# Normalisation figures computed per expert slot and carried in the rows that are read back

## The chip, the cores and the metric

One core of a Trainium2 chip runs the whole kernel. The metric is device time in microseconds (us) of one execution; lower is better.

## The reference, cut to what matters

Two layers over x of shape (4, 1024, 128), 4096 tokens of width D = 128. The change is at the joint between the first layer's mixture of experts and the second layer's attention.

```python
x = x + attention0(layernorm(x))              # 16 heads, causal, ALiBi
n = layernorm(x)                              # router and experts, E = 8, capacity C = 512 per expert
gate, idx = max(softmax(n @ Wr + br))         # top 1; a token beyond C is dropped (its gate is 0)
x = x + gate * (relu(gate * n @ W1[idx] + b1[idx]) @ W2[idx] + b2[idx])
n = layernorm(x)                              # second layer's FIRST normalisation
x = x + softmax(tanh((n Wq)(n Wk)^T / sqrt(D))) n     # among the 4 tokens of one position t
n = layernorm(x)
x = x + n @ weight.T + pooled(n) @ disha
```

Here `layernorm(x) = (x - mean) / sqrt(var + eps)`, with no learned scale.

## The kernel before

Tokens lie in 32 tiles of 128 rows, in 8 chunks of `CH = 4` tiles. The kernel has four stages; the first (attention with its router preparation, up to about 500 us) is touched only in the width of rows.

**Routing (about 500 to 562 us).** `rows` holds for each token the gated, normalised input of its expert (XG), x after the first attention (X1) and its gate (GATE): 257 words. VectorE adds the attention's output chunk by chunk (`add`), takes mean and variance (`moments`), and after GpSimd's power (`power`, variance to the power -0.5) refines the root by one Newton step (`scales`). GpSimd sends each tile's rows to their slots in DRAM (`expert_rows`) by indirect DMA (`send_rows`, L1458). SyncE stores X1 as `x1_rows` once a chunk's `add` is done, waits for all of it (`x1_out`), and loads it back as `x2` (L1428), 32 DMAs, in an order in which the four tokens that attend to each other share a tile. Then it waits until all rows are scattered, and loads the 8 experts' slots (L1431) with `es_in`.

**Experts (562 to 590 us).** For each expert, 512 slots: TensorE transposes, multiplies by W1 and W2; VectorE adds the bias into `yb` (L1576) and makes `ye = yb * gate + x1` by four instructions (L1580), so `ye` is already x after the first layer. TensorE may run two experts ahead of VectorE (`yb_ready`). SyncE stores each expert's `ye` to `expert_out` (L1435).

**Last stage (590 to 676 us).** When all eight stores have landed (`y_out`), GpSimd gathers the rows of each chunk by four indirect DMAs (`fetch`, item "g", L1469) over `x2`; a dropped token's row is not fetched and keeps x1. The items of each chunk j, in order:

- m0 (VectorE): mean and variance of the four tiles (L1589, L1592, L1595), after `y_in[j]`
- p0 (GpSimd, L1477): power; n0 (VectorE, L1601 to L1605): Newton step, shift
- a0 (ScalarE, L1898): normalised rows into `xe`, up to XE = 4 chunks ahead of "mixed"
- t3, x3, u, ut, s (TensorE and ScalarE by turns): transposes and the products of the attention; te (ScalarE): tanh and exp; mask (VectorE, L1609)
- mixed (TensorE, L1814); mix (VectorE, L1616, L1621): weighted sum added to `x2`
- m1 (VectorE), p1 (GpSimd), n1 (VectorE): the second normalisation, the same lines as m0, p0, n0 but for the shift
- t4, x4, f: transposes and the last product (L1833); add (VectorE, L1631) into `res`, which SyncE stores (L1440). f(j) waits for add(j-1)

Each engine runs its items in one fixed order, `LAST_ORDER`. It is made before the program is built by `last_plan`: a list schedule over assumed durations (`STAGES`) with random trials. Assumed on TensorE are 6.85 us for a chunk's six items, on GpSimd 5.2 us for g and 1.05 us for each power. An item at the head of an engine's order blocks what stands behind it.

TensorE also runs products whose results nobody reads (`idle_work`, L1742): 6 before the experts, 18 after them, and 6 more after the first gathered chunk has landed. In each engine's program they stand ahead of what follows:

```python
        idle_work(psS, 18)
        pe.wait_ge(y_in[0], 16 * CH)
        idle_work(psS, 6)

        def t3(j):
            pe.wait_ge(xe_ready, j + 1)
```

## Time and profile before

| | |
|---|---|
| median of 3 runs | 681.1 us (679.51 to 681.44) |
| the profiled execution | 678.24 us, with a span of 676.0 us in the profile |
| TensorE busy, share of the span | 534.4 us, 79% |
| VectorE busy | 501.2 us, 74% |
| ScalarE busy | 418.7 us, 62% |
| GpSimd busy | 234.8 us, 35% |
| mean granted TensorE clock | 0.913 of 2.4 GHz |

The span runs from the first to the last instruction and DMA of the profiled execution; the execution's own time has 2.24 us more around it. Each row of a timeline groups instructions of one line that follow each other: start, duration, engine and line, operation, written tile <- read tiles, shape and count, and in brackets the idle time before and what ended it. "early" is the buffer that holds `x2` and the router's tiles, "issue" a wait that ends with nothing that the profile shows. A clock of 1.00 is 2.4 GHz, 0.50 is 1.2 GHz.

### The profile page before, as it was taken

To read this page: it belongs to the slowest core of one execution; us is meant where nothing else is said; L and a number is where in the kernel's file an instruction comes from. 1 tells how busy PE (TensorE), PEld (TensorE's weight loads), DVE (VectorE), ACT (ScalarE), POOL (GpSimd) and SP (SyncE) were. 2 spreads that over 40 slices of the span, in tenths; PEclk is the share of its full clock that TensorE was granted. 3 is DMA by queue.
4 is the path that set the end of the run, shared out by engine and by line. 5 is a ranking of instruction groups with operands and counts; after the bars stand their busy time and mean duration, and the time that the engine had idled before them with its cause. 6 is when DMAs were issued, how large, how long until landed. Compare 5 with 4: busy or idle time off the path is not lost. (4 is left out here: it accounts for less than half of the span.)

```text
span 676.0 us, 13740 instructions
## 1 busy us (share of the span) xinstructions
PE 534.4 (79%) x4905; PEld 251.8 (37%) x4905; DVE 501.2 (74%) x1035; ACT 418.7 (62%) x737; POOL 234.8 (35%) x333
## 2 busy tenths in 40 slices
PE   3774798899999899998898888988867617957774
PEld 1441233333233223333333233333127615835563
DVE  4999878889888888789895988889008732626796
ACT  1971278787887787787786767867861412316651
POOL 2563012212212215222323224621621671078821
PEclk9886599999999999999999999989998757976897
DMA  7379355466533353121340120401013247310122
GB/s 181 88 175 280 99 128 119 116 149 196 145 83 68 67 114 67 39 42 31 68 89 19 41 56 28 121 20 37 10 25 114 71 136 284 111 28 21 35 48 63
DMA packets 66891, 61.11 MB, mean 90 GB/s; under 512 B 12121, under 2 KB 56058, under 8 KB 66812
## 3 DMA queue, kind: packets, MB, share of 16 engines
q1 hardware_dynamic: 58100, 53.93, 31.6%
q0 software_dynamic: 2560, 3.38, 1.7%
q10 hardware_dynamic: 6164, 2.94, 1.6%
q8 instruction: 39, 0.64, 0.4%
q14 instruction: 28, 0.23, 0.1%
HBM read 33.03 MB, written 29.85 MB: 93 GB/s over the span
## 5 line engine op out<-in xcount | busy, mean ns | idle before, releaser
L933 DVE TENSOR_REDUCE neg_max<-bank 128x2 f32<-128x1024 f32 (+2 forms) x320 | 341.4, 1113 | 62.8 <-PE bank L829 60.0
L973 ACT ACTIVATE probs<-ring 128x512 f32<-128x512 f32 (+4 forms) x480 | 301.8, 682 | 73.6 <-PE ring L857 62.7
L857 PE MATMUL ring<-q_operand,k_operand 56*128 56x512 bf16 (+3 forms) x768 | 161.7, 331 | 18.7 <-ACT probs L973 13.9
L878 PE MATMUL sums<-probs,v_all 128*9 128x512 f32 (+3 forms) x1536 | 161.5, 493 | 6.6 <-POOL probs L1022 4.3
L1022 POOL TENSOR_SCALAR_AFFINE_SELECT probs<-probs 128x512 f32<-128x512 f32 x128 | 80.5, 634 | 210.8 <-ACT probs L973 210.4
L829 PE MATMUL bank<-k_operand,q_operand 54*128 54x512 bf16 (+3 forms) x768 | 141.4, 340 | 9.1 <-DVE v_all L613 5.3
L857 PEld LDWEIGHTS ring<-q_operand,k_operand 56*128 56x128 bf16 x768 | 49.4, 94 | 146.0 <-ACT probs L973 103.9
L823 PE MATMUL bank<-masks 64*128 64x128 bf16 (+2 forms) x768 | 70.9, 225 | 6.8 <-DVE neg_max L933 5.8
L829 PEld LDWEIGHTS bank<-k_operand,q_operand 54*128 54x128 bf16 x768 | 46.0, 97 | 26.7 <-DVE neg_max L933 15.1
L823 PEld LDWEIGHTS bank<-masks 64*128 64x128 bf16 x768 | 36.2, 96 | 40.9 <-DVE neg_max L933 27.2
L1469 POOL DMA_INDIRECT early<-expert_out,back x32 | 32.7, 1022 | 38.3 <-issue 38.3
L878 PEld LDWEIGHTS sums<-probs,v_all 128*9 128x9 f32 x1536 | 23.5, 88 | 55.5 <-issue 42.8
L1514 DVE TENSOR_TENSOR rows<-rows,bank 128x512 f32<-128x512 f32 x6 | 4.1, 684 | 36.2 <-PE bank L1674 33.6
L980 ACT COPY max_rows_sb<-ring 32x128 bf16<-32x128 bf16 x32 | 8.0, 251 | 35.3 <-PE ring L840 35.0
L1898 ACT ACTIVATE xe<-early,nt 128x128 f32<-128x128 f32 x32 | 13.2, 482 | 24.6 <-issue 18.8
L1458 POOL DMA_INDIRECT expert_rows<-rows,early x24 | 23.6, 982 | 8.4 <-issue 6.6
L1036 POOL CAST max_parts<-low_max 128x16 bf16<-128x16 f32 x16 | 3.1, 196 | 66.4 <-DVE low_max L938 66.4
L1477 POOL TENSOR_TENSOR rs<-ve,half_pow 128x4 f32<-128x4 f32 x16 | 17.3, 1082 | 20.9 <-DVE ve L1595 20.7
L1589 DVE BATCH_NORM_STATS2 stats<-early 128x6 f32<-128x128 f32 x64 | 13.9, 279 | 14.0 <-DMA early<-expert_out,back 13.8
L986 ACT COPY osum<-sums 128x512 f32<-128x512 f32 x32 | 18.8, 588 | 7.7 <-PE sums L878 7.4
L840 PE MATMUL ring<-identb,max_parts 128*32 128x128 bf16 x32 | 7.1, 222 | 19.8 <-POOL max_parts L1039 19.1
L1856 ACT COPY early<-ring 128x512 f32<-128x512 f32 x6 | 3.5, 585 | 25.3 <-PE ring L1685 16.8
(208 smaller groups left out, 657.5 us busy)
## 6 DMA issues: line engine op xcount, KB each, us to landing
q_operand<-q_rows SPq DMA_DIRECT2D x64, 96.0 KB, 3.8
k_operand<-k_rows SPq DMA_DIRECT2D x32, 192.0 KB, 4.5
q_rows<-early SPq DMA_DIRECT2D x36, 128.0 KB, 2.4
k_rows<-early SPq DMA_DIRECT2D x36, 128.0 KB, 2.4
expert_rows<-fill SPq DMA_DIRECT2D x16, 257.0 KB, 4.2
rows<-expert_rows SPq DMA_DIRECT2D x8, 514.0 KB, 6.6
weighted_sums<-osum SPq DMA_DIRECT2D x126, 18.0 KB
sums_in<-in_L_attn_x SPq DMA_DIRECT2D x4, 512.0 KB, 7.3
```

The source lines that it names most:

```text
L823: nc.tensor.matmul(ends, masks[rows, 0, a, :], masks[rows, 1, a:a + 1, 64 * a:P].to_broadcast([64, len(pairs), P - 64 * a]), start=a == 0, ...
L829: last = nc.tensor.matmul(ps[:, h, w * j:w * j + w], q_op[rows, buf, t // CH, p, P * (t % CH):P * (t % CH) + P], k_op[rows, buf, p, CW * k ...
L857: last = nc.tensor.matmul(psS[:, bank, w * j:w * j + w], k_op[rows, buf, p, P * kb:P * kb + P], q_op[rows, buf, c, p, q0:q0 + w], start=Tr ...
L878: last = nc.tensor.matmul(psO[32 * i:32 * i + HD + 1, q0:q0 + w], v_all[:, n, kb, i, :], probs[:, u % NPROBS, i // 2, i % 2, 0:w], start=u ...
L933: nc.vector.tensor_reduce(neg_max[:, n % 2, slot, kc, :, pairs[0]:pairs[-1] + 1, t % CH], src, AX.X, ALU.max, negate=True).then_inc(a_read, 1)
L973: nc.scalar.activation(dst, src, ACT.Exp).then_inc(ring_read, 1)
L986: nc.scalar.copy(osum[:, slot, :], psO).then_inc(o_ready, 1)
L1022: nc.gpsimd.affine_select(out=tri, in_=tri, compare_op=ALU.is_ge, fill=0.0, base=0, pattern=[[0, GH], [1, P]], channel_multiplier=-1).then ...
L1458: nc.gpsimd.indirect_dma_start(out=slots_dram, out_offset=bass.IndirectOffsetOnAxis(ap=slot[:, u:u + 1], axis=0), in_=rows[:, u, :], in_of ...
L1469: nc.gpsimd.indirect_dma_start(out=x2[:, u, :], out_offset=None, in_=y_dram, in_offset=bass.IndirectOffsetOnAxis(ap=back[:, u:u + 1], axis=0),
L1477: nc.gpsimd.tensor_tensor(rs[:, z, c], ve[:, z, c], half_pow[:, 0:CH], ALU.pow).then_inc(root_ready[z], 1)
L1589: last = nc.vector.bn_stats(stats[:, z, u, :], x2[:, u, :])
```

## The change

Mean and deviation of the second layer's first normalisation are no longer taken from the gathered rows in the last stage. For a token that an expert serves, VectorE computes them in the experts' stage from `ye`, per slot, in five groups of experts (`NORMS`), with a power per group on GpSimd (`root_of_slots`); scale and shift become two more words of each `ye` row, so the stored and gathered rows are D + 2 = 130 words. For a dropped token x is unchanged by the experts, and the router's own scale and shift serve (the two norms are of the same x1): they are written into `rows` as RS and MRS, and go out and back with X1. ScalarE's a0 reads both from `x2` and waits for the gather itself. m0, p0 and n0 leave the last stage, and `last_plan` makes a new order without them. The store of X1 waits for the chunk's `scales` in place of its `add`; the load of `x2` is 4 DMAs in place of 32; a group's stores wait for the group's scales. Smaller edits that follow (`x2` by its first D columns in `mix`, `add_out`, `t4`; the logits' scale read from `rows`) are left out below.

```diff
@@ -36,7 +36,7 @@
-XG, X1, GATE, ROW = 0, D, 2 * D, 2 * D + 1
+XG, X1, RS, MRS, GATE, ROW = 0, D, 2 * D, 2 * D + 1, 2 * D + 2, 2 * D + 3
@@ -312,8 +312,8 @@
-        x1_dram = nc.dram_tensor("x1_rows", (B * S, D), F32).ap()
-        y_dram = nc.dram_tensor("expert_out", (E * CAP, D), F32).ap()
+        x1_dram = nc.dram_tensor("x1_rows", (B * S, D + 2), F32).ap()
+        y_dram = nc.dram_tensor("expert_out", (E * CAP, D + 2), F32).ap()
@@ -341,8 +341,8 @@
-            xn2=part([TILES, D]), xt2=part([2, CW]), st=part([2, CW]), rdb=part([S]),
+            x2=part([TILES, D + 2]), xt2=part([2, CW]), st=part([2, CW]), rdb=part([S]),
@@ -1074,9 +1074,9 @@
-                    e_link(nc.gpsimd.tensor_tensor(root, t, root, ALU.mult))
-                    e_link(nc.gpsimd.tensor_tensor(u, r["mv2"][:, c, 0], root, ALU.mult))
-                    nc.gpsimd.tensor_scalar(r["nt2"][:, 2, c], u, -1.0, None, ALU.mult).then_inc(scales_ready, 1)
+                    e_link(nc.gpsimd.tensor_tensor(rows[:, c, RS], t, root, ALU.mult))
+                    e_link(nc.gpsimd.tensor_tensor(u, r["mv2"][:, c, 0], rows[:, c, RS], ALU.mult))
+                    nc.gpsimd.tensor_scalar(rows[:, c, MRS], u, -1.0, None, ALU.mult).then_inc(scales_ready, 1)
@@ -1315,16 +1315,15 @@
-        nc.vector.tensor_tensor(r["nt2"][:, 0, c], r["rs2"][:, c], gate[:, c], ALU.mult)
-        nc.vector.tensor_tensor(r["nt2"][:, 1, c], r["nt2"][:, 2, c], gate[:, c], ALU.mult)
+        nc.vector.tensor_tensor(r["nt2"][:, 0, c], self.rows[:, c, RS], gate[:, c], ALU.mult)
+        nc.vector.tensor_tensor(r["nt2"][:, 1, c], self.rows[:, c, MRS], gate[:, c], ALU.mult)
...
-    STAGES = [("g", "pool", 5200, [], None), ("landed", "lag", 1500, ["g"], None), ("m0", "dve", 1450, ["landed"], None),
-              ("p0", "pool", 1050, ["m0"], None), ("n0", "dve", 700, ["p0"], None), ("a0", "act", 1650, ["n0"], ("mixed", XE)),
+    STAGES = [("g", "pool", 5200, [], None), ("landed", "lag", 1500, ["g"], None), ("a0", "act", 1650, ["landed"], ("mixed", XE)),
@@ -1358,19 +1357,19 @@
-    ye = sb("ye", [P, E, CH, D])
-    x2 = xn2
+    ye = sb("ye", [P, E, CH, D + 2])
...
-    ve, rs, nt = sb("ve1", [P, 2, TILES]), sb("rs1", [P, 2, TILES]), sb("nt1", [P, 2, 2, TILES])
+    ve, rs, nt = sb("ve1", [P, 2, TILES]), sb("rs1", [P, 2, TILES]), sb("nt1", [P, 2, TILES])
+    NORMS = [(0, 1), (2, 3), (4, 5), (6,), (7,)]
@@ -1418,20 +1417,18 @@
-            sp.wait_ge(x1_ready, k + 1)
+            sp.wait_ge(scales_ready, 1 + [k in g for g in GROUPS].index(True))
...
-                         rows[:, CH * k:CH * k + CH, X1:X1 + D]).then_inc(x1_out, 16)
+                         rows[:, CH * k:CH * k + CH, X1:X1 + D + 2]).then_inc(x1_out, 16)
         sp.wait_ge(x1_out, 16 * CHUNKS)
-        for j in range(CHUNKS):
-            for q in range(B):
-                src = x1_dram[S * q:S * q + S, :].rearrange("(u t) d -> t u d", t=32)
-                sp.dma_start(x2[32 * q:32 * q + 32, CH * j:CH * j + CH, :], src[:, CH * j:CH * j + CH, :]).then_inc(x2_in[j], 16)
+        for q in range(B):
+            sp.dma_start(x2[32 * q:32 * q + 32, :, :], x1_dram[S * q:S * q + S, :].rearrange("(u t) d -> t u d", t=32)).then_inc(x2_in, 16)
         sp.wait_ge(scattered, 16 * TILES)
...
-            sp.wait_ge(ye_ready, e + 1)
+            sp.wait_ge(ye_ready, 1 + [e in g for g in NORMS].index(True))
@@ -1464,30 +1461,35 @@
                 pool.wait_ge(y_out, 16 * E)
-            pool.wait_ge(x2_in[j], 16 * B)
+                pool.wait_ge(x2_in, 16 * B)
...
                 nc.gpsimd.indirect_dma_start(
...
-        def root(z, j):
-            pool.wait_ge(ve_ready[z], j + 1)
+        def root(j):
+            pool.wait_ge(ve_ready, j + 1)
...
-            nc.gpsimd.tensor_tensor(rs[:, z, c], ve[:, z, c], half_pow[:, 0:CH], ALU.pow).then_inc(root_ready[z], 1)
+            nc.gpsimd.tensor_tensor(rs[:, 1, c], ve[:, 1, c], half_pow[:, 0:CH], ALU.pow).then_inc(root_ready, 1)
+        def root_of_slots(g):
+            pool.wait_ge(slot_ve, g + 1)
+            c = slice(CH * NORMS[g][0], CH * NORMS[g][-1] + CH)
+            nc.gpsimd.tensor_tensor(rs[:, 0, c], ve[:, 0, c], half_pow[:, 0:CH * len(NORMS[g])], ALU.pow).then_inc(slot_roots, 1)
         for name, i in ROUTE_ORDER:
...
+        for g in range(len(NORMS)):
+            root_of_slots(g)
         for name, j in LAST_ORDER:
...
-            elif name == "p0":
-                root(0, j)
...
-                root(1, j)
+                root(j)
@@ -1518,8 +1520,8 @@
-            link(nc.vector.scalar_tensor_tensor(rs2[:, c], nt2[:, 1, c], 1.5, rs2[:, c], ALU.add, ALU.mult))
-            nc.vector.scalar_tensor_tensor(nt2[:, 2, c], mv2[:, c, 0], -1.0, rs2[:, c],
+            link(nc.vector.scalar_tensor_tensor(rows[:, c, RS], nt2[:, 1, c], 1.5, rs2[:, c], ALU.add, ALU.mult))
+            nc.vector.scalar_tensor_tensor(rows[:, c, MRS], mv2[:, c, 0], -1.0, rows[:, c, RS],
@@ -1571,38 +1573,70 @@
-        for e in range(E):
+        def expert_sum(e):
             dve.wait_ge(y_psum, e + 1)
...
                                     b2b[:, e:e + 1, :].to_broadcast([P, CH, D]), ALU.add).then_inc(yb_ready, 1)
             dve.wait_ge(yb_ready, e + 1)
...
-                last = nc.vector.scalar_tensor_tensor(ye[:, e, a, :], yb[:, e % 2, a, :], es[:, e, a, GATE:GATE + 1],
+                last = nc.vector.scalar_tensor_tensor(ye[:, e, a, 0:D], yb[:, e % 2, a, :], es[:, e, a, GATE:GATE + 1],
...
-            last.then_inc(ye_ready, 1)
-        def moments(z, j):
+            last.then_inc(ye_sum, 1)
+        def slot_moments(e):
+            dve.wait_ge(ye_sum, e + 1)
+            for a in range(CH):
+                last = nc.vector.bn_stats(stats[:, 0, CH * e + a, :], ye[:, e, a, 0:D])
+            link(last)
+            for a in range(CH):
+                last = nc.vector.bn_aggr(mv[:, 0, CH * e + a, :], stats[:, 0, CH * e + a, :])
+            link(last)
+        def slot_variances(g):
+            c = slice(CH * NORMS[g][0], CH * NORMS[g][-1] + CH)
+            nc.vector.tensor_scalar_add(ve[:, 0, c], mv[:, 0, c, 1], EPS).then_inc(slot_ve, 1)
+        def slot_scales(g):
+            dve.wait_ge(slot_roots, g + 1)
+            es_of = slice(NORMS[g][0], NORMS[g][-1] + 1)
+            c = slice(CH * NORMS[g][0], CH * NORMS[g][-1] + CH)
+            v, r, t = ve[:, 0, c], rs[:, 0, c], nt[:, 0, c]
+            by_slot = lambda x: x.rearrange("p (e a) -> p e a", a=CH)
+            scale, shift = ye[:, es_of, :, D], ye[:, es_of, :, D + 1]
+            link(nc.vector.scalar_tensor_tensor(t, v, -0.5, r, ALU.mult, ALU.mult))
+            link(nc.vector.tensor_tensor(t, t, r, ALU.mult))
+            link(nc.vector.scalar_tensor_tensor(scale, by_slot(t), 1.5, by_slot(r), ALU.add, ALU.mult))
+            nc.vector.scalar_tensor_tensor(shift, by_slot(mv[:, 0, c, 0]), -1.0, scale, ALU.mult, ALU.mult).then_inc(ye_ready, 1)
+        for g, group in enumerate(NORMS):
+            for e in group:
+                expert_sum(e)
+                slot_moments(e)
+                if e == group[0] and g > 0:
+                    slot_scales(g - 1)
+            slot_variances(g)
+        slot_scales(len(NORMS) - 1)
+        def moments(j):
...
-                last = nc.vector.bn_stats(stats[:, z, u, :], x2[:, u, :])
+                last = nc.vector.bn_stats(stats[:, 1, u, :], x2[:, u, 0:D])
...
-                last = nc.vector.bn_aggr(mv[:, z, u, :], stats[:, z, u, :])
+                last = nc.vector.bn_aggr(mv[:, 1, u, :], stats[:, 1, u, :])
...
-            nc.vector.tensor_scalar_add(ve[:, z, t], mv[:, z, t, 1], EPS).then_inc(ve_ready[z], 1)
-        def scales_of(z, j):
-            dve.wait_ge(root_ready[z], j + 1)
+            nc.vector.tensor_scalar_add(ve[:, 1, t], mv[:, 1, t, 1], EPS).then_inc(ve_ready, 1)
+        def scales_of(j):
+            dve.wait_ge(root_ready, j + 1)
...
-            v, r, t = ve[:, z, c], rs[:, z, c], nt[:, z, 0, c]
+            v, r, t = ve[:, 1, c], rs[:, 1, c], nt[:, 1, c]
...
-            if z == 0:
-                nc.vector.scalar_tensor_tensor(nt[:, z, 1, c], mv[:, z, c, 0], -1.0, t, ALU.mult, ALU.mult).then_inc(nt_ready, 1)
@@ -1890,13 +1919,13 @@
-            act.wait_ge(nt_ready, j + 1)
+            act.wait_ge(y_in[j], 16 * CH)
...
-                last = nc.scalar.activation(xe[:, j % XE, i, 0:D], x2[:, u, :], ACT.Identity, bias=nt[:, 0, 1, u:u + 1],
-                                            scale=nt[:, 0, 0, u:u + 1])
+                last = nc.scalar.activation(xe[:, j % XE, i, 0:D], x2[:, u, 0:D], ACT.Identity, bias=x2[:, u, D + 1:D + 2],
+                                            scale=x2[:, u, D:D + 1])
...

```

## Rows read from the trace of the kernel before

**Rows 1.** Windows by stage: width, busy us (instructions) of each engine, granted clock, DMA.

```profile
560.00:590.30 30.30, 27.93 (x151) 22.14 (x152) 14.70 (x42) 10.07 (x16) 0.92 (x1) 0.91 0.56 212
590.30:640.60 50.30, 34.34 (x157) 25.18 (x155) 25.89 (x145) 22.62 (x48) 41.27 (x41) 0.76 0.12 28
640.60:676.00 35.40, 21.39 (x138) 17.55 (x138) 28.66 (x144) 13.04 (x26) 8.69 (x8) 0.88 0.23 53
```

**Rows 2.** Timeline of VectorE (DVE), experts' stage: start, duration, line, instructions.

```profile
571.07 0.69 DVE L1576 TENSOR_TENSOR yb<-ring,b2b 128x512 f32<-128x512 f32 x1 [7.21 <-PE ring L1767]
...
573.25 0.69 DVE L1576 TENSOR_TENSOR yb<-ring,b2b 128x512 f32<-128x512 f32 x1 [0.32 <-PE ring L1767]
...
585.57 0.68 DVE L1576 TENSOR_TENSOR yb<-ring,b2b 128x512 f32<-128x512 f32 x1
586.29 1.14 DVE L1580 SCALAR_TENSOR_TENSOR ye<-yb,rows 128x128 f32<-128x128 f32 x4
```

**Rows 3.** Timeline of GpSimd (POOL), last stage: gathers (L1469) and powers (L1477).

```profile
590.32 1.05 POOL L1469 DMA_INDIRECT early<-expert_out,back  x1 [29.40 <-issue]
...
595.59 1.00 POOL L1469 DMA_INDIRECT early<-expert_out,back  x1 [0.30 <-issue]
...
638.22 1.00 POOL L1469 DMA_INDIRECT early<-expert_out,back  x1 [0.31 <-issue]
...
647.88 1.38 POOL L1477 TENSOR_TENSOR rs<-ve,half_pow 128x4 f32<-128x4 f32 x1 [4.07 <-DVE ve L1595]
```

**Rows 4.** Waits of VectorE from 590.3 to 640.6: total us, times, longest.

```profile
DVE stats L1589 <- DMA early<-expert_out,back: 13.8, 2, 9.3
DVE nt L1601 <- POOL rs L1477: 10.6, 6, 3.3
```

**Rows 5.** Timeline of VectorE, end of the last stage.

```profile
653.75 1.12 DVE L1631 SCALAR_TENSOR_TENSOR res<-ring,nt,early 128x128 f32<-128x128 f32 x4
654.80 0.68 DVE L1609 TENSOR_TENSOR ee<-ee,samet 128x512 f32<-128x512 f32 x1
...
658.22 0.15 DVE L1601 SCALAR_TENSOR_TENSOR nt<-ve,rs 128x4 f32<-128x4 f32 x1
...
658.84 1.13 DVE L1631 SCALAR_TENSOR_TENSOR res<-ring,nt,early 128x128 f32<-128x128 f32 x4
...
671.35 1.12 DVE L1631 SCALAR_TENSOR_TENSOR res<-ring,nt,early 128x128 f32<-128x128 f32 x4 [0.74 <-PE ring L1833]
```

**Rows 6.** Timeline of VectorE, first chunk of the last stage.

```profile
596.76 0.87 DVE L1589 BATCH_NORM_STATS2 stats<-early 128x6 f32<-128x128 f32 x4 [9.33 <-DMA early<-expert_out,back]
...
598.09 0.17 DVE L1595 TENSOR_SCALAR ve<-mv 128x4 f32<-128x4 f32 x1
601.58 0.16 DVE L1601 SCALAR_TENSOR_TENSOR nt<-ve,rs 128x4 f32<-128x4 f32 x1 [3.32 <-POOL rs L1477]
...
602.25 0.86 DVE L1589 BATCH_NORM_STATS2 stats<-early 128x6 f32<-128x128 f32 x4
```

**Rows 7.** Timeline of SyncE's DMA queue: issues with their span.

```profile
542.15 19.14 SPq L1428 DMA_DIRECT2D early<-x_rows  x32
562.12 4.13 SPq L1431 DMA_DIRECT2D rows<-expert_rows  x8
```

**Rows 8.** Timeline of ScalarE (ACT), first chunk of the last stage.

```profile
602.37 1.65 ACT L1898 ACTIVATE xe<-early,nt 128x128 f32<-128x128 f32 x4 [18.81 <-issue]
```

**Rows 9.** Timeline of TensorE (PE), last stage.

```profile
596.78 5.49 PE L1742 MATMUL bank<-sel,ident 128*128 128x256 f32 x12 [4.25 <-DMA early<-expert_out,back]
...
607.33 2.07 PE L1804 MATMUL bank<-ut,xt 128*128 128x128 f32 x8 [0.68 <-issue]
...
612.49 1.07 PE L1814 MATMUL ring<-xe,ee 128*128 128x129 f32 x4
...
624.16 1.13 PE L1804 MATMUL bank<-ut,xt 128*128 128x128 f32 x8 [0.30 <-ACT th L1919]
```

**Rows 10.** Window of TensorE in the last stage: width, busy, granted clock, DMA.

```profile
606.00:608.00 2.00, 1.32 (x5) 0.57 0.14 33
```

More of the change, by code:

```diff
@@ L1275, in scaled @@
         n = c.stop - c.start
-        self.link(dve, nc.vector.tensor_tensor(lg, z, r["rs2"][:, c].unsqueeze(2).to_broadcast([P, n, E]), ALU.mult))
+        self.link(dve, nc.vector.tensor_tensor(lg, z, self.rows[:, c, RS].unsqueeze(2).to_broadcast([P, n, E]), ALU.mult))
         self.link(dve, nc.vector.tensor_tensor(lg, lg, w["brb"][:, :].unsqueeze(1).to_broadcast([P, n, E]), ALU.add))
@@ L1360, in later_stages @@
     at = sb("at", [P, 2, CW])
-    xn2, xt2, mv2, ve2, rs2, nt2, lg, ex, gate, slot, pos = (
-        r[k] for k in ("xn2", "xt2", "mv2", "ve2", "rs2", "nt2", "lg", "ex", "gate", "slot", "pos"))
+    x2, xt2, mv2, ve2, rs2, nt2, lg, ex, gate, slot, pos = (
+        r[k] for k in ("x2", "xt2", "mv2", "ve2", "rs2", "nt2", "lg", "ex", "gate", "slot", "pos"))
     router, place_counts = shared["router"], shared["place_counts"]
@@ L1392, in later_stages @@
         sem(n) for n in ("g_psum", "xgt_ready", "z_psum", "hid_ready", "y_psum", "yb_ready", "ye_ready", "y_out"))
-    x2_in, y_in = ([sem(f"{n}{j}") for j in range(CHUNKS)] for n in ("x2_in", "y_in"))
+    x2_in, slot_roots = sem("x2_in"), sem("slot_roots")
+    y_in = [sem(f"y_in{j}") for j in range(CHUNKS)]
     back_psum, back_ready = sem("back_psum"), sem("back_ready")
     fold_psum, fold_ready = sem("fold_psum"), sem("fold_ready")
-    ve_ready, nt_ready = [sem(f"ve_ready{i}") for i in range(2)], sem("nt_ready")
-    root_ready = [sem(f"root_ready{i}") for i in range(2)]
+    ve_ready, root_ready, slot_ve, ye_sum = sem("ve_ready"), sem("root_ready"), sem("slot_ve"), sem("ye_sum")
     xe_ready, t3_psum, xt3_ready, u_psum, ut_ready = (sem(n) for n in ("xe_ready", "t3_psum", "xt3_ready", "u_psum", "ut_ready"))
@@ L1620, in mix @@
                 c0 = (i % 2) * (CW // 2)
-                last = nc.vector.scalar_tensor_tensor(x2[:, u, :], psMix[i // 2][:, c0:c0 + D], inv[:, u:u + 1],
-                                                      x2[:, u, :], ALU.mult, ALU.add)
+                last = nc.vector.scalar_tensor_tensor(x2[:, u, 0:D], psMix[i // 2][:, c0:c0 + D], inv[:, u:u + 1],
+                                                      x2[:, u, 0:D], ALU.mult, ALU.add)
             last.then_inc(x3_ready, 1)
@@ L1630, in add_out @@
                 u = CH * j + i
-                last = nc.vector.scalar_tensor_tensor(res[:, j % 2, i, :], psOut[:, P * i:P * i + P], nt[:, 1, 0, u:u + 1],
-                                                      x2[:, u, :], ALU.mult, ALU.add)
+                last = nc.vector.scalar_tensor_tensor(res[:, j % 2, i, :], psOut[:, P * i:P * i + P], nt[:, 1, u:u + 1],
+                                                      x2[:, u, 0:D], ALU.mult, ALU.add)
             last.then_inc(res_ready, 1)
         for name, j in LAST_ORDER:
-            if name == "m0":
-                dve.wait_ge(y_in[j], 16 * CH)
-                moments(0, j)
-            elif name == "n0":
-                scales_of(0, j)
-            elif name == "n1":
-                scales_of(1, j)
+            if name == "n1":
+                scales_of(j)
             elif name == "mask":
@@ L1648, in _ @@
                 dve.wait_ge(x3_ready, j + 1)
-                moments(1, j)
+                moments(j)
             elif name == "add":
@@ L1822, in t4 @@
             for i in range(CH):
-                last = nc.tensor.transpose(psT4[:, P * i:P * i + P], x2[:, CH * j + i, :], ident[:, :])
+                last = nc.tensor.transpose(psT4[:, P * i:P * i + P], x2[:, CH * j + i, 0:D], ident[:, :])
             last.then_inc(t4_psum, 1)
```

4 lines of the change are left out of this document (2 added, 2 removed).

## The prediction

> **What bounds the kernel now.** I read first the windows by stage [rows 1]. The change touches the last two of them most: the experts' stage (to 590.3) and the last stage, which falls into a part with the gathers (to 640.6) and one after them. In the experts' stage TensorE is busy 27.93 of 30.30 us. In the gathers' part GpSimd is the busiest, 41.27 of 50.30, and VectorE has 25.89. After them VectorE has 28.66 of 35.40.
>
> Then the timelines, to see who waits. In the experts' stage VectorE starts at 571.07 and is back every 2.18 us, of which 0.32 is a wait for TensorE's last product [rows 2]: TensorE sets the pace, VectorE has 0.3 us of room per expert. The last `ye` ends at 587.43, and GpSimd's first gather starts at 590.32, 2.89 later, which is the last store [rows 2, 3].
>
> In the gathers' part GpSimd goes on without a pause: four gathers take 5.27 us, 1.32 each, and the last of 32 starts at 638.22 [rows 3]. That is 47.9 after the first, of which 31 x 1.32 = 40.8 are gathers and 7.1 are the seven powers among them, 1.0 each. VectorE waits here: 13.8 us for gathered rows in m0, 10.6 us for powers in n0 and n1 [rows 4]. So it has a backlog when the last rows land. From there it goes almost without a pause: add 1.05, then mask, mix and m1 3.42, then n1 0.62, in sum 5.09 a chunk [rows 5]. The last add ends at 672.47, and the stores bring the end, at 676.0, 3.5 later. The end is thus set by: last store of the experts, 32 gathers, VectorE's backlog.
>
> **What the change does before the experts.** X1 is stored after `scales` in place of `add`; from the first chunk's rows the way from m0 to the end of n0 is 5.6 us, a good bound for that delay [rows 6]. The 4 DMAs then issue far faster than the 32, which took 19.14 us of SyncE's queue from 542.15 to 561.3 [rows 7]. Behind them on the queue are only the experts' loads, issued at 562.12 when the scatter is done. If the data of the 4 loads need half the old 19.1 us they end about 557, and cost nothing; if they need all of it and start 5.6 late, they end at 566.9 and the experts' first load comes up to 5 us late, part of which TensorE's padding products there cover. I take nothing, and keep +3 for a rival. The Trainium skill (DMA: Bandwidth & Descriptors, How a descriptor splits into AXI transactions) says that a run not starting at a 256 B boundary costs extra beats, and 520-byte rows mostly do not; from its beats I would estimate some 25% on these loads, which the cover holds, and no row of before shows rows of 520 bytes. The 128 columns of VectorE's and ScalarE's tiles are as before, and two words more in a row of 257 are under 1%: nothing.
>
> **What it adds to the experts' stage.** Per expert, VectorE now spends 0.72 on `yb`, 1.14 on the four `ye`, 0.03 on its own semaphore, and then the moments of four tiles, which m0 shows at 1.33 (596.76 to 598.09) [rows 2, 6]. That is 3.22 against TensorE's 2.18, so VectorE sets the pace from its start at 571.07, with TensorE two experts ahead. Eight experts: 25.8 us, to 596.9. Five variance additions (at most 0.17 each, mostly overlapped): 0.5. Four sets of scales inside the loop at 0.67 (601.58 to 602.25): 2.7; their powers are done during the expert between. That makes 600.1. Then the last group, exposed: a power of 1.2 with its hops (between 1.0 and the 1.38 of [rows 3]), to 601.3, and four scale instructions, 0.8, to 602.1. With the same 2.89 for the store the first gather starts at 605.0, against 590.32: **14.7 us later**. Bounds: 13.5 (no own-semaphore gaps, short power) to 16.
>
> **What it takes from the last stage.** I count from the first gather, F. Before, the end is F + 85.7. Eight times m0 and n0 are 8 x (1.33 + 0.67) = 16 us of VectorE, and eight powers 8 of GpSimd; the long waits of VectorE [rows 4] lie mostly on them. The last rows now land at F + 43.3 plus 1.0 for each p1 that stands among the gathers (32 x 1.32, less the last gap, plus the 1.4 that the first chunk took to land: 590.32 to 596.76 less 5.0). With one or two p1 that is 44.8.
>
> The first chunk gets a new wait. The six padding products after `y_in[0]` ran from 596.78 to 602.27, beside m0, p0, n0 and a0, which ended at 604.02: they cost nothing [rows 8, 9]. Now only a0 (1.65) covers them, and the first t3 starts at F + 12, 3.8 us after its data. At the full clock they would take half, and 1.1 us would stay; but TensorE was idle for 4.25 before them and ran them at the half clock, and now it is idle longer. In the queue behind them is all of TensorE's work; GpSimd is not, so the gathers run on, and only as much of it remains as VectorE cannot make up.
>
> A chunk takes from the start of a0 to the end of m1: before, 602.37 to 613.56 for the last product of mixed, and mix and m1 2.8 more: 14.0 at the half clock (1.2 GHz); 12 at the full one (2.4 GHz), as s falls from 2.07 to 1.13 and mixed by as much [rows 8, 9]. Chunk j starts at F + 6.4 + 5.27 j. When the last rows land at 44.8, chunks 0 to 4 have mask, mix and m1 behind them and chunk 5 has mask and mix: 5 x 3.42 + 2.0 = 19.1 us of VectorE's work, with one or two pairs of n1 and add 21.6. Of 8 x 5.09 = 40.7 there remain 19.1. I add 2.5 for waits in this part (before, 31.9 us passed for 28.66 of work, some of it in the gaps that 5.09 holds) and the 3.5 of the stores: F + 69.9, and I take **F + 70.2** for an order that doesn't quite fit. This is the widest term: the new order is unknown to me, and a p1 must pass GpSimd's blocks of 5.2 us.
>
> **The sum**: 605.0 + 70.2 = 675.2 against the span of 676.0, a gain of 0.8 us: the 14.7 us added ahead of the gathers eat the 15.5 saved behind them. The profiled execution took 678.24, 2.24 over its span, and the median of the runs is 681.1; I carry the difference over, **680.3**. A change of under 0.3%, 2.0 us, can't be told from none in this kernel.
>
> **The rivals.** *Faster*: the order puts three or four p1 among the gathers, and VectorE keeps up, since it needs 5.09 a chunk and the gathers come every 5.27 or slower. Then the last chunk alone sets the end: its a0 starts at F + 46.3, m1 ends 12 later, p1, n1 and add take 3.1, the stores 3.5: 64.9, and 1.5 for meeting other chunks: 66.4. End 671.4, 4.6 less: 676.5. For it speaks that VectorE's waits on m0 and n0 go; against it that the seven powers before were let in only when due, and that a schedule which thinks TensorE the bound has no reason to serve p1 early.
>
> *Slower, by TensorE's clock*: in the window from 606 to 608 TensorE was busy 1.32 of 2.00 us and fell to the half clock with one chunk in work [rows 10]. After the change it works a new chunk every 5.3 us, with waits between. At the half clock the four items of a chunk that lead to mix (t3, u, s, mixed) take by my estimate 3.5 times s, 7.2 against 3.9 (s is 2.07 or 1.13 [rows 9]), more than the 5.27 of the gathers: 1.9 late per chunk. It decides from the third such chunk on: 5.8 late, some 2 of it made up, so 679 or 680, 3.5 to 4 more than the forecast's end: 684. Against it: after 640.6 TensorE was busy 21.39 of 35.40 and had a mean clock of 0.88 [rows 1]. The Trainium skill (TensorE: Matmul & The Clock Gate, HAM oscillation) has a rule for this: products in short bursts between waits for DMA restart cold each time. By that rule alone the half clock would stay through the gathers and this rival would hold; the trace agrees with it only in part, as the clock did rise later in the gathers' part, whose mean is 0.76.
>
> *Slower, by the loads of* `x2`: they land late, +3: 683.3; only if the four loads move their rows no faster than the thirty-two did, and start late besides.
>
> **How the numbers follow.** Forecast 0.40, with its own range 678 to 682.5 (the bounds of the experts' term, and one or two chunks' n1 and add more or less done at the landing); faster rival 0.31; clock 0.21; loads 0.08. The range reaches from 674.5 to 685. Faster by over 0.3% (below 679.1): 0.31 and a quarter of the forecast's, less a little for half-hearted cases, 0.40; slower (above 683.1): 0.28; the rest, 0.32, is the same.
>
> **What would show it.** In the profile after: VectorE's period in the experts' stage 3.2 to 3.6 us with no wait for TensorE; the first gather at 604 to 606; 12 padding records that end after a0 of chunk 0, and t3 behind them; the last gather at F + 42 to 45; VectorE's work after it, 19 us with the waits small. It would be wrong if VectorE's added work overlapped in the experts' stage better than its durations add up, if the new order stalls VectorE or TensorE behind a gather, or if the clock differs from what is said. It is most exposed in the last: an error of one chunk's work is 5 us, more than the whole difference.

## The result and the profile after

The changed kernel takes **694.1 us** (median of 4 runs, 692.4 to 696.0); the kernel before took 681.3 on the same chip. The ratio is **1.0214** (95% interval 1.0186 to 1.0241): 2.1% slower, above the range of the prediction. The profiled execution has a span of 690.3 us.

The part that the change adds came as forecast. VectorE in the experts' stage after; compare [rows 2] and [rows 6]:

```profile
568.88 0.69 DVE L1578 TENSOR_TENSOR yb<-ring,b2b 128x512 f32<-128x512 f32 x1 [7.86 <-PE ring L1796]
569.61 1.14 DVE L1582 SCALAR_TENSOR_TENSOR ye<-yb,rows 128x128 f32<-128x128 f32 x4
570.78 0.87 DVE L1589 BATCH_NORM_STATS2 stats<-ye 128x6 f32<-128x128 f32 x4
...
572.11 0.69 DVE L1578 TENSOR_TENSOR yb<-ring,b2b 128x512 f32<-128x512 f32 x1
...
599.59 0.17 DVE L1610 SCALAR_TENSOR_TENSOR ye<-mv,ye 128x4 f32<-128x4 f32 x1
```

An expert takes 3.23 us, without a wait for TensorE. GpSimd's first gather starts at 602.68, 33.80 us after the first `yb`, against 19.25 before [rows 2, 3]: 14.55 later, where I had 14.7.

The part that the change should shorten got longer. Windows after, cut at the first gather and at the end of the last one, as [rows 1]:

```profile
602.70:649.30 46.60, 26.29 (x112) 19.80 (x112) 7.55 (x33) 16.33 (x35) 33.46 (x33) 0.69 0.12 24
649.30:690.30 41.00, 27.14 (x172) 21.78 (x172) 31.50 (x151) 18.43 (x37) 8.24 (x8) 0.87 0.23 53
```

VectorE is busy only 7.55 us while the gathers run (25.89 before) and has 31.50 left afterwards, where I had reckoned 19.1 and some gaps. From the first gather to the end it takes 87.6 us, against 85.7 before and a forecast of 70.2. Who let VectorE wait is in its waits after, from 602 to 690:

```profile
DVE ee L1643 <- ACT ee L1953: 22.1, 3, 20.7
DVE inv L1650 <- remote: 18.0, 2, 13.4
```

The 20.7 is the first chunk's way to mask, which must be. The 13.4 is new: VectorE waits for the first mixed product, and the trace names no instruction that let it go ("remote"). The timelines of VectorE, ScalarE and TensorE around it:

```profile
620.46 0.69 DVE L1643 TENSOR_TENSOR ee<-ee,samet 128x512 f32<-128x512 f32 x1 [20.70 <-ACT ee L1953]
634.58 0.17 DVE L1650 RECIPROCAL inv<-bank 128x2 f32<-128x2 f32 x1 [13.43 <-remote]
```

```profile
636.75 0.60 ACT L1948 ACTIVATE th<-bank 128x512 f32<-128x512 f32 x1 [9.96 <-remote]
```

```profile
625.20 1.07 PE L1843 MATMUL ring<-xe,ee 128*128 128x129 f32 x4
626.06 1.91 PE L1833 MATMUL bank<-ut,xt 128*128 128x128 f32 x8
627.77 0.95 PE L1819 MATMUL bank<-ident,xe 128*128 128x128 f32 x4
636.03 1.12 PE L1852 MATMUL ring<-ident,early 128*128 128x128 f32 x4 [7.32 <-DVE early L1655]
```

By the records mixed of chunk 0 (L1843) ended at 626.27 and s of chunk 1 (L1833) at 627.97. VectorE learned of the first at 634.58, 8.3 us late, ScalarE of the second at 636.75, 8.8 late. I call this a **held signal**: a consumer idle until "remote", though the product it waits for is recorded as ended.

"Remote" says more than that: the trace also has the time of each update of a semaphore, and the word stands where such an update ended the wait and no instruction that makes it had ended near it. The update for mixed of chunk 0 stands at 634.55, the one for s of chunk 1 at 636.73. So the consumers started at once, and the updates themselves were late. Only TensorE's are: from 500 us on, those of ScalarE, VectorE and GpSimd stand within 0.04 us of their instructions' ends in all the traces here, beside the same gathers. GpSimd meanwhile:

```profile
602.68 1.11 POOL L1466 DMA_INDIRECT early<-expert_out,back  x1 [3.72 <-issue]
...
632.78 1.00 POOL L1466 DMA_INDIRECT early<-expert_out,back  x1 [0.30 <-issue]
637.59 1.05 POOL L1474 TENSOR_TENSOR rs<-ve,half_pow 128x4 f32<-128x4 f32 x1 [3.81 <-DVE ve L1631]
```

From 602.68 to 633.78 it issued 24 gathers with 0.30 us between them. Before, a power p0 (L1477) stood behind every fourth or eighth [rows 3]. The change took p0 out, and the two signals came 0.8 and 3 us behind the end of that run.

### The profile page after: what moved, and what is told of

Same layout as the page of the kernel before. It is cut to its first block and busy times, and to the rows that moved or that the text cites. A ratio compares the mean times of both kernels' runs of the same rounds, so it can differ in the third digit from the quotient of the medians.

```text
span 690.3 us, 13701 instructions
## 1 busy us (share of the span) xinstructions
PE 533.3 (77%) x4905; PEld 250.7 (36%) x4905; DVE 499.4 (72%) x1020; ACT 417.9 (61%) x737; POOL 234.1 (34%) x330
## 5 line engine op out<-in xcount | busy, mean ns | idle before, releaser
L857 PE MATMUL ring<-q_operand,k_operand 56*128 56x512 bf16 (+3 forms) x768 | 161.0, 330 | 19.1 <-ACT probs L973 13.9
L1927 ACT ACTIVATE xe<-early 128x128 f32<-128x128 f32 x32 | 13.2, 486 | 26.4 <-DMA early<-expert_out,back 26.4
L1036 POOL CAST max_parts<-low_max 128x16 bf16<-128x16 f32 x16 | 3.2, 197 | 66.4 <-DVE low_max L938 66.4
L1771 PE MATMUL bank<-sel,ident 128*128 128x256 f32 x48 | 14.3, 469 | 11.4 <-DMA early<-expert_out,back 11.4
L840 PE MATMUL ring<-identb,max_parts 128*32 128x128 bf16 x32 | 7.1, 222 | 19.7 <-POOL max_parts L1039 19.1
L1643 DVE TENSOR_TENSOR ee<-ee,samet 128x512 f32<-128x512 f32 x8 | 5.5, 687 | 22.1 <-ACT ee L1953 22.1
L1474 POOL TENSOR_TENSOR rs<-ve,half_pow 128x4 f32<-128x4 f32 x8 | 9.3, 1157 | 29.6 <-DVE ve L1631 29.6
```

The lines of the kernel that those rows point to most:

```text
L857: last = nc.tensor.matmul(psS[:, bank, w * j:w * j + w], k_op[rows, buf, p, P * kb:P * kb + P], q_op[rows, buf, c, p, q0:q0 + w], start=Tr ...
L1771: nc.tensor.matmul(bank[:, CW // 2:], ident[:, :], sel[:, 0:2, :].rearrange("p c m -> p (c m)"), start=True, stop=True)
L1927: last = nc.scalar.activation(xe[:, j % XE, i, 0:D], x2[:, u, 0:D], ACT.Identity, bias=x2[:, u, D + 1:D + 2], scale=x2[:, u, D:D + 1])
```

## The experiments

**Theory S**: TensorE's signals are held while GpSimd issues indirect DMAs without a pause, and p0 had been the pause. **Rivals**: **O**, the newly planned order of the last stage; **C**, TensorE's half clock and the padding products behind `y_in[0]`. Ratios are to the kernel before. "Stage" is the time from the first gather to the end, "held" the sum of VectorE's and ScalarE's waits that end in "remote" in it (whole waits, so it can be more than the signals were late), "runs" the gathers between pauses of at least 0.9 us in their issue. Of 'after' they are 87.6, 32.8 and 24, 8; of the kernel before 85.7, 2.4 and 8, 8, 4, 4, 4, 4.

The experiments ran in five batches, each on a chip of its own with the kernel before beside it: e1 to e4 on chip 13, e5 to e8 on 10, e9 to e12 on 4, e13 to e16 on 9, e17 and e18 on 12. The chip matters, as will be seen.

**Pauses in the changed kernel, and the two rivals alone.**

```python
            if name == "g":
                fetch(j)
                nc.gpsimd.tensor_tensor(brk[...], brk[...], half_pow[:, 0:CH], ALU.pow)   # e1
...
-        pe.wait_ge(y_in[0], 16 * CH)      # e2
-        idle_work(psS, 6)
...
-LAST_ORDER = last_plan()                 # e3: before's order, less m0, p0, n0
```

> The changed kernel with one extra GpSimd power on 4 scratch columns behind each chunk's 4 gathers (8 in all, about 1.05 us each). Theory S (held signals): TensorE's finish signals reach VectorE and ScalarE late while GpSimd issues indirect DMAs without a break, and the change made one run of 24 gathers out of runs of at most 8 to 10. With runs of 4 the wait of 13.4 us before the first reciprocal of the mix (VectorE, L1650) falls to 3 to 7 us, that of te(1) on ScalarE goes, and the time falls from 694 to 684 to 689 us, though GpSimd has 8 us more to do. Theory O (the new order of the last stage) and theory C (TensorE at half clock, uncovered padding): the waits stay, the gathers end up to 8 us later, 694 to 699 us.

> The changed kernel without the wait of TensorE for the first rows and the six padding products behind it. Theory C: t3(0) comes 3 to 4 us earlier, and if the products' time is what the first chunk lacks, the time falls by 3 to 4 us to 690 to 691 us. Theory S: mixed(0) may end earlier, but its signal is still held to the end of the run of gathers at F+31, so the time stays within 1.5 us of 694.

> The changed kernel with the last stage's order of the kernel before (without its m0, p0 and n0) in place of the newly planned one. Theory O: the planned order costs most of the 17 us, so the time falls to 680 to 684 us. Theory S: the first run of gathers has 20 in place of 24 and ends 5 us earlier, so the held signal of mixed(0) comes about 5 us earlier; 689 to 692 us.

Measured: e1 **1.0146** (1.0103 to 1.0189), e2 **1.0280** (1.0229 to 1.0330), e3 **1.0346** (1.0306 to 1.0387). VectorE at the same two places in e1:

```profile
621.74 0.69 DVE L1648 TENSOR_TENSOR ee<-ee,samet 128x512 f32<-128x512 f32 x1 [20.56 <-issue]
624.29 0.17 DVE L1655 RECIPROCAL inv<-bank 128x2 f32<-128x2 f32 x1 [1.86 <-PE ring L1848]
```

The wait of 13.43 is 1.86, with no held signal in the stage (81.1 us), although GpSimd has 8.4 us more to do. Neither rival gains anything alone: e2's interval overlaps that of the change (1.0186 to 1.0241), e3 lies above it. In e3, where the first run has 20 gathers and the second 12, another signal is held:

```profile
650.59 1.13 DVE L1674 SCALAR_TENSOR_TENSOR res<-ring,nt,early 128x128 f32<-128x128 f32 x4 [17.75 <-remote]
```

The product of this wait is recorded as ended at 644.56 and its update stands at 650.48, 5.9 us later; the rest of the 17.75 is the work before it, which had been held too. I had expected e3 to gain some us by its shorter first run; it lost another 9.

**The reverse, on the kernel before.** Both kernels put 1.0 in place of the root of the first normalisation, which is what their output leaves out.

```python
             elif name == "p0":
-                root(0, j)                                                  # e4: nothing here
+                nc.gpsimd.tensor_tensor(brk[...], brk[...], half_pow[:, 0:CH], ALU.pow)   # e9
```

> The kernel before with the eight powers of the first normalisation left out on GpSimd (VectorE takes 1.0 in place of the root; the sum of products is then wrong by that part, nothing else is left out). This takes 8.4 us from GpSimd and a round trip from each chunk. Without theory S: 2 to 5 us faster than before (676 to 679 us). Theory S: the gathers now stand in one run of 20 or more as in the changed kernel, the waits for TensorE's signals grow to 8 us or more, and the time is 681 to 690 us, no faster or slower than before although work was taken away.

> The kernel before with the root of the first normalisation replaced by 1.0 as in the run without its powers (the product is wrong by that part), but with a power of the same size on scratch columns where each p0 stood, which waits for nothing. GpSimd has the work and the breaks of the kernel before, without the round trip. Theory S2: the gathers stand in runs of at most 12 between pauses of 1 us again, and the 1.3% that leaving the powers out had cost is gone: 674 to 680 us against 679.5 of the kernel before, its last stage (first gather to end) 80 to 86 us in place of 95.4. If it was the earlier gathers or the missing round trip that cost the time, and not the missing pause, it stays at 685 to 690 us.

Measured: e4 **1.0127** (1.0088 to 1.0165), e9 **1.0025** (0.9997 to 1.0053). Taking GpSimd's eight powers out, work and round trip both, makes the kernel before slower: stage 95.4, held 27.0. With a power on scratch, which nobody waits for, the time is that of the kernel before: 86.8, held 0.0. But e9 ran on chip 4, where, as shown below, no signal was held in any kernel; it can't show that its powers freed anything, and e4 has no control on its own chip but the kernel before. VectorE in e4:

```profile
621.18 0.17 DVE L1618 RECIPROCAL inv<-bank 128x2 f32<-128x2 f32 x1 [4.40 <-remote]
...
640.29 0.17 DVE L1618 RECIPROCAL inv<-bank 128x2 f32<-128x2 f32 x1 [6.26 <-remote]
```

**How long a pause, and how many.** In the changed kernel a memset of one column, and a power behind chunk 4 only:

```python
                fetch(j)
+                nc.gpsimd.memset(brk[:, 0, j:j + 1], 1.0)      # e5; e8: in fetch, behind every gather
...
+                if j == 4:                                     # e6
+                    nc.gpsimd.tensor_tensor(brk[...], brk[...], half_pow[:, 0:CH], ALU.pow)
```

> As the run with a power behind each chunk's gathers, but the break is a memset of one column (about 0.1 us) in place of a power of 1.05 us. If any other instruction of GpSimd lets the held signals through (S1), mix(0) starts within 3 us of mask(0)'s end, as with the powers, and since GpSimd has 7.5 us less to do the time falls to 683 to 688 us. If it is the pause of about 1 us in the issue of transfers that does it (S2), mix(0) waits 8 to 13 us as in the changed kernel, and the time is 692 to 696 us.

> A memset of one column behind every gather (32 in all), otherwise the changed kernel. S1 (any other GpSimd instruction lets the signals through): no wait for TensorE's signals is longer than 2.5 us, GpSimd gets 3 to 6 us longer, time 684 to 689 us. S2 (a pause of about 1 us is needed): waits of 8 us and more remain, 694 to 699 us.

> The changed kernel with a single power on scratch columns, behind the gathers of chunk 4 (runs of 20, 4 and 8 gathers). Theory S: the power stands at about F+26 to F+27 (F is the start of the first gather), so mix(0) starts at F+27 to F+28.5 in place of F+31.9, and the time falls by 3 to 5 us to 689 to 692 us. Theories without S: mix(0) does not move against mixed(0)'s end, time 694 to 696 us.

Measured: e5 **1.0226** (1.0196 to 1.0257), e8 **1.0249** (1.0230 to 1.0267), e6 **1.0226** (1.0204 to 1.0248). The memset of 0.11 us fits into the 0.30 us that lie between two gathers anyway, as GpSimd's timeline of e5 shows:

```profile
612.29 1.00 POOL L1467 DMA_INDIRECT early<-expert_out,back  x1 [0.30 <-issue]
613.29 0.11 POOL L1495 MEMSET brk<- 128x1 f32 x1
613.59 1.00 POOL L1467 DMA_INDIRECT early<-expert_out,back  x1 [0.19 <-issue]
```

e5 differs from e1 by that instruction alone (in place of a power of 1.05 us), and both chips hold signals. So another instruction is not enough; the issue must pause. In e6 the power stood at 631.00 to 632.05 and mix(0) started at 633.30, F + 28.2, as forecast, against F + 31.9 after the change; but nothing was gained. One pause doesn't free all that is held: s of chunk 1 and t3 of chunk 2 had ended at 627.98 and 628.42, before the power, and their updates stand at 638.96 and 641.79, behind the next one. VectorE's next mix waited 7.3 us more.

**The order, with pauses.** The last stage is planned anew with 6.25 us for a chunk's gathers instead of 5.2; e13 has this order and no pause.

```python
-    STAGES = [("g", "pool", 5200, [], None), ...      # e7, e10, e12, e13; e14 keeps 5200
+    STAGES = [("g", "pool", 6250, [], None), ...
...
                fetch(j)
+                nc.gpsimd.tensor_tensor(brk[...], ..., ALU.pow)     # e7; e12, also without the padding
+                nc.gpsimd.memset(brk[...], 1.0)                     # e10, e14: 256 columns, 0.33 us
```

> Powers as breaks behind each chunk's gathers, and the last stage's order planned anew with 6.25 us in place of 5.2 us for a chunk's gathers. The held signals gone, what is left is the order: VectorE waits 8.0 us for ee and 4.3 us for roots after 624 in the run with the breaks alone. If order O matters beside S, 683 to 686 us; if not, 688 to 689 us as with the breaks alone.

> The replanned kernel with its breaks, without the wait of TensorE for the first rows and the padding products behind it. With the signals no longer held, t3(0) comes 3 to 4 us after a0(0)'s rows instead of behind the products. Theory C: the first chunk gains 3 to 4 us and the time falls to 679 to 681 us. If the later chunks are bound by GpSimd's gathers (6.25 us each, to F+50) and VectorE, or the clock falls for want of the products, it stays at 682 to 685 us.

> The replanned kernel with the breaks shortened from 1.05 us to a memset of 256 columns, estimated at 0.55 us (512 columns took 1.005 us, one column 0.11 us). If half a microsecond of pause is enough, no wait for TensorE's signals over 3 us, GpSimd ends 4 us earlier, and 679 to 683 us against 683.2. If it needs about 1 us, the waits of 8 us and more are back and it takes 688 to 695 us.

> The replanned order of the last stage alone, with no break between the gathers: runs of 24, 4 and 4 gathers as in the changed kernel. If the pauses do it (S), the wait for mixed(0) or a later product of 8 us or more is back and the time is 688 to 697 us (ratio to the kernel before 1.012 to 1.025). If it is the order (O), no such wait, and the time is that of the run with the short breaks, 674 to 678 us (ratio 0.995 to 1.002).

> The changed kernel's own order with the short breaks (a memset of 256 columns, 0.33 us, which waits for the one before it). S: mix(0) waits under 3 us instead of 13.4, and since GpSimd has 5.8 us less in breaks than with the powers (ratio 1.0146), the ratio to the kernel before is 1.002 to 1.010. If the order was what the replanned runs gained by, the waits stay and the ratio is 1.018 to 1.025.

Measured: e7 **1.0067** (1.0035 to 1.0099), e12 **1.0106** (1.0057 to 1.0155), e10 **0.9972** (0.9945 to 1.0000), e13 **1.0233** (1.0183 to 1.0282), e14 **1.0233** (1.0181 to 1.0286).

With pauses the order is worth 5.8 us of the stage (81.1 in e1, 75.3 in e7); without them it is worth nothing (e13: 90.7, held 24.6). So O holds only behind S. Taking the padding products out gains nothing in either setting: C falls in that part. e10's stage is 69.3 us with no held signal, within 1 us of the 70.2 that I had forecast for the change, though with another order and on chip 4. Against e12 on the same chip (75.2, without the padding products) it is 5.9 less, and its eight pauses take 8 x (1.05 - 0.33) = 5.8 less of GpSimd: that gain is saved work, not freed signals. Its waits of VectorE, to be set against those of after:

```profile
DVE ee L1649 <- ACT ee L1959: 20.3, 1, 20.3
DVE inv L1656 <- PE ring L1849: 5.4, 3, 2.3
DVE nt L1643 <- POOL rs L1475: 1.3, 1, 1.3
```

e14 shows the late signals best, as they start there under the full clock. Its window, then ScalarE:

```profile
624.80:632.60 7.80, 4.05 (x26) 3.15 (x26) 3.61 (x16) 3.77 (x8) 6.37 (x7) 1.00 0.13 26
```

```profile
631.35 0.60 ACT L1954 ACTIVATE th<-bank 128x512 f32<-128x512 f32 x1 [2.78 <-remote]
...
634.23 0.59 ACT L1944 COPY xt<-bank 128x512 f32<-128x512 f32 x1 [1.63 <-remote]
...
637.08 0.59 ACT L1964 COPY xt<-ring 128x512 f32<-128x512 f32 x1 [2.26 <-remote]
```

The three products that these wait for are recorded at 627.13 to 629.71, one behind the other; their updates stand at 631.33, 634.21 and 637.06, 2.9 us apart, in order. At the next pause of GpSimd (its last gather of that run ended at 651.66) they come at once. TensorE, then the two that waited:

```profile
647.57 0.61 PE L1849 MATMUL ring<-xe,ee 128*128 128x129 f32 x4
648.02 1.05 PE L1839 MATMUL bank<-ut,xt 128*128 128x128 f32 x8
```

```profile
652.89 0.17 DVE L1656 RECIPROCAL inv<-bank 128x2 f32<-128x2 f32 x1 [6.59 <-remote]
```

```profile
652.98 0.60 ACT L1954 ACTIVATE th<-bank 128x512 f32<-128x512 f32 x1 [1.69 <-remote]
```

The second product alone is eight matmuls, 1.05 us; the two signals are 0.09 us apart. In the changed kernel four updates stand at 650.34, 650.43, 650.53 and 650.59, for products recorded as ended from 645.86 to 648.58. So the products were done and the news of them was late, not TensorE slow. The Trainium skill (Perfetto Trace Analysis, Tensor Engine Instruction) fits with it: TensorE's end in a trace is an estimate, and the update is pushed only when PSUM has acknowledged the writes, and then has to spread. It gives no delay of microseconds, and no tie to GpSimd; the runs show both.

**Fewer and shorter pauses, and the chip.** e15 is e10, and e16 the kernel before, with one memset among the routing's scatters. e11, e17 and e18 are e7 with fewer powers.

```python
             send_rows(u):
+                if u == KB + 3:                           # e15, e16
+                    nc.gpsimd.memset(rest[:, :], 1.0)
...
                fetch(j)
+                if j % 2 == 1:      # e11; e17: j in (1, 3); e18: j == 3
+                    nc.gpsimd.tensor_tensor(brk[...], ..., ALU.pow)
```

> The replanned kernel with short breaks, and one more memset of 256 columns behind the fourth of the eight scatters that GpSimd issues in a row in the routing part (525 to 536 us in the kernel before, where ScalarE waited 8.5 us at L1856 and VectorE 2.5 us at L1514 for signals of TensorE). S: those waits fall by 3 to 5 us, of which 0 to 3 us reach the end, since the second half of the routing is bound by GpSimd's 16 scatters: ratio 0.993 to 0.998.

> The kernel before with that one memset of 256 columns behind the fourth of the eight scatters, and nothing else changed. S: the waits of 8.5 us (ScalarE, L1856) and 2.5 us (VectorE, L1514) for signals of TensorE at 537 us fall by 3 to 5 us; ratio 0.995 to 1.000. Without S: the waits stay, and the scatters come 0.3 us later.

> The replanned kernel with powers only behind chunks 1, 3, 5 and 7: runs of 8 gathers, as the kernel before had at most, in place of 4. Theory S2: a signal can now be held up to 10 us; GpSimd has 4.2 us less. Where the signals of the first two chunks fall decides; 683 to 690 us, with one to three waits of 3 to 8 us for TensorE's signals.

> The replanned order with powers of 1.05 us as breaks behind chunks 1 and 3 alone: GpSimd's own powers p1 follow from chunk 5 on, so no run has more than 8 gathers. Theory S2 (what counts is that a pause of about 1.2 us comes at least every 8 to 12 gathers): no wait for held signals, and 2 us less of GpSimd than with breaks behind chunks 1, 3, 5 and 7 (ratio 1.0016): ratio 0.996 to 1.001. If every further pause was needed, a hold is back and the ratio is over 1.005.

> The same with one power, behind chunk 3: runs of 16, 8, 4 and 4 gathers. The first chunk's signals that were held in the runs of 20 and 24 fall at F+18 to F+25 (F is the start of the first gather), just about this break at F+21, so if pauses only free what is held, the holds are short: 0 to 4 us in sum, ratio 0.996 to 1.006. If a hold, once begun in a long run, goes on behind the pause, waits of 8 us or more are back and the ratio is 1.010 to 1.025.

Measured: e15 **1.0179** (1.0141 to 1.0218), e16 **1.0009** (0.9985 to 1.0033), e11 **1.0016** (0.9990 to 1.0042), e17 **1.0125** (1.0084 to 1.0166), e18 **1.0251** (1.0207 to 1.0295). The memset among the routing's scatters frees nothing (ScalarE's wait of 8.5 us is 8.5 in both). e15, which differs from e10 by that one instruction and its tile, has held signals again: ScalarE, 9.00 us to 633.84. It also ran on another chip, and the routing tells which of the two counts. There ScalarE waits beside eight scatters that the change and the experiments leave alone (but for two words more in a row, and e15's and e16's memset); the kernel before, then e10:

```profile
537.15 0.58 ACT L1856 COPY early<-ring 128x512 f32<-128x512 f32 x1 [8.49 <-remote]
```

```profile
532.09 0.59 ACT L1891 COPY early<-ring 128x512 f32<-128x512 f32 x1 [3.17 <-PE ring L1720]
```

In all sixteen traces of the other chips this wait is 8.3 to 8.6 us and ends in "remote"; in the four of chip 4 (e9 to e12) it is 3.1 to 3.6 and ends with the product. From 500 us on, not one of TensorE's updates in those four traces is over 0.05 us behind its product; in each of the sixteen, 8 to 17 are over 0.3 us behind, e1 and e7 with them in the routing. So chip 4, or its batch, doesn't hold signals whatever the kernel issues. All last stages together:

| pauses in the gathers | kernels | longest run | held, us | latest update, us behind its product |
|---|---|---|---|---|
| 1.2 us behind every 4 | e1, e7 | 4 | 0, 0 | 1.2, 0.5 |
| 1.2 us or more, runs up to 8 | before, e16, e17 | 8 | 2.4, 2.4, 8.1 | 2.8, 2.8, 4.6 |
| 0.49 us behind every 4 | e14, e15 | 24 | 30.9, 11.5 | 7.3, 11.8 |
| longer runs | after, e2, e3, e4, e5, e6, e8, e13, e18 | 16 to 24 | 32.8, 34.3, 31.5, 27.0, 25.6, 35.5, 35.7, 24.6, 12.9 | 7.5 to 17.6 |
| any, on chip 4 | e9, e10, e11, e12 | 4 to 24 | 0, 0, 0, 0 | 0.02 |

The last row bears on no theory of pauses. So e10 doesn't show that 0.49 us is enough, and where signals are held it was not (e14, e15). Nor do e11 and e17 contradict each other: e17, which leaves out e11's two last powers and has no longer run, lost on chip 12 what e11 kept on chip 4. I took them for the same test. e17's profiled execution was the shortest of its six, 682.7 us against a median of 686.4. No version beats the kernel before by more than the measurement can tell: e10, at 0.9972, is the best, and how it does on another chip is not known, but e15 is it with one memset more, at 1.0179.

Two things stay untested. The changed kernel itself, and any kernel with a run of 24 and no pause, never ran on chip 4. And every execution on record was traced, as each has its span and clock, so the tracing itself may take part. One sign for that: of the 512 updates that the 32 gathers make, the traces of chip 4 have 506 to 512, the others 159 to 340.

## Why the prediction was wrong

**Before the experts: nothing lost.** The four loads of `x2` took 4.94 us of SyncE's queue where the 32 took 19.14 [rows 7], and the experts' loads went out at 559.45 (562.12 before). The first `yb` came at 568.88, 2.2 earlier; over the runs here it lies between 568.7 and 574.5 with nearly the same code ahead of it, so I give the change no credit for that. The rival of late loads falls.

**The experts' stage: right**, 14.55 for 14.7.

**The first chunk: right up to mask.** The padding products (12 records, 5.49 us) and t3 at F + 11.9 came as forecast (F + 12).

**The step that failed** is "a chunk takes from the start of a0 to the end of m1 ... 12 to 14 us", and with it that five chunks have mask, mix and m1 behind them when the last rows land. Chunk 0 took from 609.29 to 637.5, 28.2 us, of which 13.4 are the held signal; by the last gather's end two chunks were that far, and a second hold followed at 650.4. In e10, where nothing is held, chunk 0 took 16.4 us and chunk 1 14.2, and VectorE had done 21.6 us of work by the last gather's end, the amount that I had forecast; after the change it was 7.55. I had named a stall "behind a gather" among what would make me wrong, but had priced none. I took GpSimd's powers for work and a round trip to be saved; their third part, a pause in the gathers, I didn't see. It could be seen: the kernel before has such a wait beside its run of eight scatters in the routing, ScalarE's 8.49 us to 537.15 shown above.

**The sum.** The span was forecast at 675.2 and came at 690.3. The earlier start is -2.3 (602.68 for 605.0), the last stage +17.4 (87.6 for 70.2), together +15.1. Of the 17.4, pauses of 1.05 us give back 6.5 net of their own 8.4 us of GpSimd (e1), the order behind them 5.8 (e7), shorter pauses 6.0 (e10, on the chip without holds). The changed kernel's own order without holds and without long pauses was never seen, as e14 had holds, so how the 17.4 divides between holds and order in it stays open.

**The rival of TensorE's clock** had its sign right (684) but not its cause. The granted clock was 0.69 in the gathers' part (0.76 before [rows 1]). The holds of e14 began at a clock of 1.00, though, and in e10, without holds, the clock was 0.88 in the gathers' part as far as 644.6:

```profile
602.90:644.60 41.70, 29.42 (x168) 22.43 (x168) 16.73 (x77) 23.94 (x52) 34.12 (x38) 0.88 0.14 32
```

So the holds are not an effect of the half clock. Some of the low clock follows from them: in the change's first hold TensorE was busy 0.72 of 8.00 us (628 to 636), and the clock was 0.50 from 636 to 640. It was 0.50 from 624 to 628 already, before that hold, so not all of it does. The Trainium skill's rule that I had used for this rival (TensorE: Matmul & The Clock Gate, HAM oscillation) is on products in short bursts between waits for DMA. e10 doesn't meet that condition, as TensorE waited for DMA once, 10.0 us for the first rows, and never over 1.0 us after that; so its clock neither bears the rule out nor speaks against it. The faster rival was open only to a kernel without holds: e10's 69.3 lies between its 66.4 and the forecast's 70.2.

## What to carry to other kernels

An instruction that is taken off an engine may have served as a pause for what the engine does around it: before moving work away from between indirect DMAs, look for waits that end in "remote" on consumers of TensorE, and at what GpSimd issues beside them. Where they appear, about 1 us of other GpSimd work behind every four transfers (a pause of 1.2 us) kept them away in this stage (e1, e7), at a cost in GpSimd's time; plan the order with it. Run a variant and its control on the same chip, and look at a wait that neither of them touches: here such a wait (ScalarE's in the routing) shows that e9, e10 and e11 could not test what they were made for. A saving that rests on an engine's busy time alone isn't safe when the order of several engines is planned anew.

## What was not expected of the hardware

While GpSimd issued 16 or more gathers of 128 rows with at most 0.3 us between them, updates of TensorE's semaphores came up to 17.6 us behind the recorded end of their product (e2: 629.11, update at 646.72), and the consumers' waits for them sum to 12.9 to 35.7 us per execution, in nine kernels of nine, none of them on chip 4. The updates of ScalarE, VectorE and GpSimd were on time (within 0.04 us) all the while. With pauses of 1.2 us behind every four gathers no consumer waited for a held one, in two kernels of two on chips that hold them; with pauses of 0.49 us they did, in two of two. In the four kernels of chip 4 TensorE's updates were never over 0.05 us late, neither in this stage nor in the routing.

Held updates come out in order: beside gathers 2.1 to 4.2 us apart in e2, e3 and e14 and 12 us in e13, and behind the last gather those still held come within 0.3 to 2.7 us, mostly 0.05 to 0.1 us apart. What starts a hold is open: in e14 all updates of chunk 0 up to mixed (product 627.29, update 627.31) were on time beside the same gathers. Whether it is the chip, something in its batch or the tracing that decides if signals are held at all is open too. That other indirect DMAs do the same is only seen in the routing (8.5 us of waiting beside eight scatters), where the one short pause tried did not help.
